# Combining only the two chosen experts of an image, fetched from a table in HBM at addresses computed on the chip

## The chip, the core and the metric

One Trainium2 chip, one of its NeuronCores. The kernel is one launch; its metric is the device time of that launch in microseconds (us). The engines of the core run their own instruction lists and meet only at semaphores: TensorE (PE, with its weight loads shown as PEld), VectorE (DVE), ScalarE (ACT), GpSimd (POOL) and SyncE (SP), whose list holds almost nothing but DMA issues.

## The reference

Input x is 32 images of 32x32 pixels and 64 channels, float32. Two blocks follow one another, each `x = x + block(group_norm(x))`.

```
for t in range(3):                        # block 1: routed convolution, three steps
    attn    = softmax(q . (x Wk)) over pixels, 2 heads
    logits  = pooled(attn, x Wv) @ Wmlp    # 4 experts
    weights = softmax(where(allowed, logits, -1e9) / 1.5)
    top     = the 2 largest of the 4;  wsel = weights of the top 2, normalised, 0 for the others
    x_mod   = x * (1 + mean attention map * 1024 * softplus(alpha))
    x       = sum over e of wsel[e] * (conv3x3(x_mod, We[e]) + be[e])
    allowed = allowed minus the first choice (expert 3 stays allowed)
# block 2: per pixel a 3x3 kernel for each of 16 channel groups from a 64->16 projection, applied to x Wi + bi
```

Since a convolution is linear in its weights, the sum over experts can be formed on the weights first: one combined 3x3x64x64 kernel per image and step, two of whose four terms are zero.

## The kernel before

All 32 images stay in SBUF, two to a tile of 128 partitions (a pair). Four images, that is two pairs, make a quad. A step of the routed block takes 8 quads, cut into two phases of 4 quads, so that there are 6 phases p and 24 quads q = 4p + j. One pass of the main loop does, for quad q: the 3x3 convolution on PE, meanwhile on the other engines the combined weights of quad q+1, its modulated and padded input, and piece by piece the attention and the routing of phase p+1.

Quads 4, 6, 8, 10, 12 and 14 (`SHORT`) use a row transform with 4 forms of the kernel's rows in place of 3 and save a third of the matmuls; their combined weights are 4 blocks of 192 columns (768), those of the others 9 taps of 64 (576). PSUM has two units for the convolution (`conv`, halves h = 0 and 1) and two for everything beside it (`att`).

The combination works as follows. `experts` (128 x 4 x 768) holds the weights of the four experts in both halves of the partitions. `begin_combine(q)` on ACT (L839 to L858) writes expert 0 times its weight into `comb[q % 2]`, once for each pair n; it first waits until the convolution of quad q-2 has read that buffer. `combine(q)` on DVE (L1260 to L1278) adds experts 1, 2 and 3: six `scalar_tensor_tensor`. In a quad with j = 3 behind a short one (`hurried`) DVE also does the first product of pair 0 itself. `comb_added` counts the additions; the convolution waits for them.

The order on each engine is the order of the code. On ACT a pass is: `begin_combine(q+1)`, the exponentials of phase p+1 if j = 0, `copy_middle(q)` if q is short, `round_attention` if j = 2 or 3, then the emptying of the convolution's PSUM. On DVE (L1433 to L1480): `combine(q+1)`, `row_max` and `weigh` if j = 0, `middle_rows(q)` if q is short, `reduce_attention` if j = 3, `modulate(q+1)`, `finish_rows(q, 0)`, and the sums and differences of rows if q+1 is short. The last stage of attention for the next phase (`attention_map` on PE, (3, 1, 2)) waits for `parts_ready`, which ACT raises at the end of `round_attention`.

The routing of phases 0 and 1 is done on DVE (`route`, L1133), that of phases 2 to 5 on POOL (`route_beside`, L1576), one short dependent instruction after the other. SP is idle between the loading of the inputs and the constants of the second block (L388), which it issues when quad 18 has been modulated.

## Time and profile before

| | |
|---|---|
| device time, three runs | 682.75, 683.7, 683.96 us; median 683.7 |
| profiled execution, first to last instruction | 680.8 us |
| granted TensorE clock, mean over the span | 0.985 |
| PE / DVE / ACT / POOL busy | 649.5 / 553.8 / 285.0 / 172.3 us |

The profile gives no separate total of its execution: its span of 680.8 us is 2.9 us below the median of the runs, which is what lies before the first and after the last instruction together with the scatter of single runs. In time the kernel falls in four parts: loading, first norm and routing (0 to about 60 us), quads 0 to 3 (to 130), quads 4 to 23 (to 459), and the second block (to 681). Times of day in the rows are microseconds from the start of the span.

### The profile page before, as it was taken

Reading aid. Unit: us, or ns where it says so; the run is one execution under the profiler, and the core shown is the slowest. Engines: PE = TensorE matmul, PEld = TensorE weight load, DVE = VectorE, ACT = ScalarE, POOL = GpSimd, SP = SyncE. Lnnn points to the kernel's source line nnn. Section 1 sums busy time; section 2 is a strip of 40 time slices with the busy share of each in tenths; the row PEclk is TensorE's granted clock in tenths of the full one; section 3 lists DMA queues with packets and bytes.
Section 4 is the critical chain, followed back from the end, with each engine's and each line's share of the span. In section 5 each row is a group of like instructions: output and inputs, shape, how many; then the busy total and the mean of one; then the engine's idle time right before and its main releaser. Section 6 shows DMA issues by size and latency. Waiting matters only on the chain.

```text
span 680.8 us, 14823 instructions
## 1 busy us (share of the span) xinstructions
PE 649.5 (95%) x6176; PEld 268.1 (39%) x6176; DVE 553.8 (81%) x904; ACT 285.0 (42%) x367; POOL 172.3 (25%) x156
## 2 busy tenths in 40 slices
PE   7878999999999999999999999999999999999995
PEld 7433333333333333333333334433445444444442
DVE  5698866989988988995577787849888888888885
ACT  3753622322331322133002411033676777777661
POOL 2100310009102800550051110411353243244230
PEclk9979999999999999999999999998999999999998
DMA  9920000000000000000000000000111211121122
GB/s 332 213 56 1 2 1 1 1 1 2 2 1 1 2 1 1 2 1 1 1 14 2 1 1 2 1 1 1 32 33 32 58 37 33 45 49 33 32 62 63
DMA packets 54511, 19.67 MB, mean 29 GB/s; under 512 B 51154, under 2 KB 51892, under 8 KB 54452
## 3 DMA queue, kind: packets, MB, share of 16 engines
q1 hardware_dynamic: 54164, 18.57, 11.2%
q8 instruction: 49, 0.80, 0.5%
q10 hardware_dynamic: 288, 0.21, 0.1%
q14 instruction: 10, 0.08, 0.0%
HBM read 10.39 MB, written 8.39 MB: 28 GB/s over the span
## 4 chain that ended last, share of the span: by engine, by line
PE 74%; DVE 15%; issue 1%; ACT 1%; DVEq 0%; ACTq 0%
PE conv L675 35%; PE att L745 11%; PE conv L729 10%; PE att L465 4%; PE conv L641 4%; PE att L544 4%; DVE xpad L1188 3%; DVE comb L1277 2%; PE att L717 2%; DVE stats L1291 2%; PE att L556 2%; DVE x L1497 2%; PE att L523 1%; DVE x L1246 1%; DVE x L1253 1%
## 5 line engine op out<-in xcount | busy, mean ns | idle before, releaser
L675 PE MATMUL conv<-xpad,comb 64*64 64x512 f32 x2592 | 290.3, 595 | 3.1 <-DVE x L1253 2.9
L1497 DVE TENSOR_TENSOR x<-conv,x 128x512 f32<-128x512 f32 x288 | 179.2, 683 | 26.4 <-PE conv L729 25.0
L675 PEld LDWEIGHTS conv<-xpad,comb 64*64 64x64 f32 x2592 | 99.3, 134 | 170.1 <-issue 159.4
L1277 DVE SCALAR_TENSOR_TENSOR comb<-experts,wsel,comb 128x576 f32<-128x576 f32 (+1 forms) x138 | 113.5, 888 | 5.2 <-ACT comb L857 4.8
L729 PE MATMUL conv<-rstack,wse 98*128 98x512 f32 x288 | 96.2, 444 | 1.9 <-DVE xin L1286 0.9
L857 ACT ACTIVATE comb<-experts,wsel 128x576 f32<-128x576 f32 (+2 forms) x49 | 35.2, 768 | 108.5 <-PE conv L675 69.7
L745 PE MATMUL att<-x,cmp 64*32 64x512 f32 x1280 | 79.7, 596 | 0.0
L729 PEld LDWEIGHTS conv<-rstack,wse 98*128 98x128 f32 x288 | 49.5, 189 | 60.7 <-DVE x L1497 46.2
L1188 DVE SCALAR_TENSOR_TENSOR xpad<-att,x 128x1024 f32<-128x1024 f32 x46 | 54.0, 1215 | 20.8 <-PE att L523 20.6
L1634 POOL TENSOR_TENSOR x<-x,xin 128x1024 f32<-128x1024 f32 x15 | 35.9, 2396 | 115.1 <-ACT x L997 115.1
L867 ACT ACTIVATE x<-conv,bias 128x512 f32<-128x512 f32 x40 | 25.2, 680 | 84.0 <-PE conv L675 84.0
L1573 POOL TENSOR_TENSOR rt<-rt 128x16 f32<-128x16 f32 x12 | 6.9, 579 | 199.3 <-ACT rt L837 198.7
L977 ACT ACTIVATE x<-att,small 64x512 f32<-64x512 f32 x64 | 44.0, 687 | 12.6 <-PE att L556 12.0
L1291 DVE BATCH_NORM_STATS2 stats<-xin 128x6 f32<-128x512 f32 x64 | 43.5, 680 | 2.8 <-ACT xin L820 1.4
L1627 POOL TENSOR_TENSOR rstack<-x,rstack 32x1024 fp32r<-32x1024 f32 x16 | 38.1, 2383 | 28.9 <-ACT rstack L989 28.9
L1286 DVE SCALAR_TENSOR_TENSOR xin<-conv,bias,xin 128x512 f32<-128x512 f32 x32 | 22.5, 744 | 26.4 <-PE conv L675 26.1
L997 ACT ACTIVATE x<-att 64x512 f32<-64x512 f32 x60 | 35.5, 592 | 15.8 <-PE att L745 14.7
L641 PE MATMUL conv<-row_sums,comb 64*64 64x512 f32 x288 | 33.3, 591 | 1.3 <-DVE row_sums L1222 1.3
L641 PE MATMUL conv<-xpad,comb 64*64 64x512 f32 x288 | 33.6, 596 | 0.0
L745 PEld LDWEIGHTS att<-x,cmp 64*32 64x32 f32 x1280 | 18.5, 106 | 34.2 <-issue 33.0
L544 PE MATMUL att<-x,wr 128*96 128x512 f32 x64 | 31.5, 615 | 0.0
L1004 ACT ACTIVATE comb<-att 128x1024 f32<-128x1024 f32 x15 | 15.4, 1027 | 31.1 <-PE att L717 31.1
(187 smaller groups left out, 611.4 us busy)
## 6 DMA issues: line engine op xcount, KB each, us to landing
x<-in_x SPq DMA_DIRECT2D x32, 256.0 KB, 5.1
out<-comb SPq DMA_DIRECT2D x30, 256.0 KB, 3.2
experts<-in_We SPq DMA_DIRECT2D x1, 1152.0 KB
out<-comb SPq DMA_DIRECT2D x4, 128.0 KB, 2.2
wide<-in_c_wide SPq DMA_DIRECT2D x1, 192.0 KB, 5.9
x<-in_c_sum SPq DMA_DIRECT2D x1, 160.0 KB
small<-in_c_small ACTq DMA_DIRECT2D x1, 142.5 KB, 3.8
map_sel<-in_c_map SPq DMA_DIRECT2D x1, 128.0 KB
```

The costliest lines, as they stand in the source:

```text
L544: last = nc.tensor.matmul(att[0:rows, 1, cols], weights, xn[s][:, cols], start=True, stop=True)
L641: last = nc.tensor.matmul(conv[own[to], h, HW * rows:HW * rows + HW], comb[own[rows], q % 2, n, form * ROW + kw * C:form * ROW + kw * C + ...
L675: last = nc.tensor.matmul(conv[own[to], h, HW * rows:HW * rows + HW], comb[own[rows], q % 2, n, tap(t)], xpad[own[rows], 2 * (q % 2) + n, ...
L729: nc.tensor.matmul(conv[:, unit, cols], wse[:, ORDER[i], :], rstk[s][0:RR, cols], start=True, stop=True).then_inc(exp_full, 1)
L745: last = nc.tensor.matmul(att[q, 0, bank], sum_sel[own_rows, t + upper, :], prod[i][own_rows, cols], start=(r == 0), stop=(r == len(ROUNDS ...
L977: done = nc.scalar.activation(xip[s][own[n], 1 + 16 * h:17 + 16 * h, 1:W + 1], att[rows, 1, bank].rearrange("p (a b) -> p a b", b=W), ACT. ...
L1188: v.scalar_tensor_tensor(inner(q, n), img(att[:, use.unit, :]), 1.0, img(x[:, slot(q, n), :]), ALU.add, ALU.mult).then_inc(att_free[use.un ...
L1277: v.scalar_tensor_tensor(comb[:, q % 2, n, cols], experts[:, e, cols], wsel[:, p % 2, j + QP * n, e:e + 1], comb[:, q % 2, n, cols], ALU.m ...
L1291: gn.then(v.bn_stats(stats[:, k, n, :], xin[:, k, n * HW:(n + 1) * HW]))
L1497: v.tensor_tensor(img(prod[i])[:, rows, :], img(conv[:, unit, :])[:, rows, :], xip[s][:, kh + 16 * h:kh + 16 * h + 16, kw:kw + W], ALU.mul ...
L1627: v.tensor_tensor(rstk[s][32:64, :], r96[32:64, :], rstk[s][32:64, :].bitcast(F32), ALU.subtract)\
L1634: v.tensor_tensor(fin, fin, xin[:, k, :], ALU.add).then_inc(fin_ready, 1)
```

## The change

From quad 5 on (`GATHER_FROM`) DVE and ACT combine two experts per image and not four.

- POOL computes one more block of rows (`minus_forms`), and SP writes all forms of all four experts into a table `forms` in HBM, 7 blocks of 192 columns for each expert, in three DMAs.
- The routing also gives, for each image, the numbers of its first and second choice (`top_at`, int32) and their weights (`top_weight`): `pick_experts(1)` on DVE for phase 1, new lines in `route_beside` on POOL for phases 2 to 5.
- `gather(q)` on SP: for each of the 4 images of the quad and each of its 2 choices, `value_load` reads the number from SBUF into a register, and a DMA with that address fetches 64 partitions x 576 (or 768) floats into `chosen`, the same memory as `experts`. It overwrites what the quad before used, so it waits for that quad's additions.
- ACT's product waits for the DMAs of its pair and reads the first choice; DVE adds the second: 2 `scalar_tensor_tensor` per quad in place of 6. In short quads the form that DVE used to subtract (`minus_ready`) comes ready from the table.

```
+        top_at = packed(small, 0, 2 * GP * TOP).bitcast(mybir.dt.int32).rearrange("p (a i r) -> p a i r", a=2, r=TOP)
+        chosen = experts[:, :, :].rearrange("p (n r) c -> p n r c", n=2)
+        forms = nc.dram_tensor("forms", (K, C, FORM_BLOCKS * ROW), F32, kind="Internal")
...
+        def added(q):
+            return (K - 1) * (2 + min(q, GATHER_FROM - 1) + 1) + max(0, q - GATHER_FROM + 1)
...
+            def write_forms():
+                eng.wait_ge(forms_ready, 4)
+                table = forms[:, :, :].rearrange("k p c -> p k c")
+                eng.dma_start(table[:, :, 4 * ROW:7 * ROW], experts[0:C, :, 0:3 * ROW]).then_inc(forms_out, 16)
+                eng.dma_start(table[:, :, ROW:4 * ROW], experts[0:C, :, ROW:4 * ROW]).then_inc(forms_out, 16)
+                eng.dma_start(table[:, :, 0:ROW], minus_forms[0:C, :, :]).then_inc(forms_out, 16)
+            def gather(q):
+                p, j = divmod(q, QP)
+                if j == 0 or q == GATHER_FROM:
+                    eng.wait_ge(top_ready, p)
+                first, size = (0, 4 * ROW) if q in SHORT else (4 * ROW, TAPS * C)
+                for n in range(2):
+                    if q == GATHER_FROM:
+                        for m in range(2):
+                            eng.wait_ge(comb_added[m], added(q - 1))
+                    else:
+                        eng.wait_ge(comb_added[n], added(q - 1))
+                    for m in range(2):
+                        for r in range(TOP):
+                            at = eng.value_load(top_at[64 * m:64 * m + 1, p % 2, j + QP * n, r:r + 1], min_val=0, max_val=K - 1)
+                            eng.dma_start(chosen[own[m], n, r, 0:size],
+                                          forms[bass.ds(at, 1), :, first:first + size].rearrange("k p c -> (k p) c")).then_inc(gathered[n], 16)
+            write_forms()
+            eng.wait_ge(forms_out, 16 * FORMS_WRITTEN)
+            for q in range(GATHER_FROM, QP * LAST + 4):
+                gather(q)
             modulated(eng, QP * LAST + 2)
             for dst, src in LATE_CONSTS:
                 eng.dma_start(dst, src).then_inc(late_consts_in, 16)
+            for q in range(QP * LAST + 4, QUADS):
+                gather(q)
...
                 for cols in taps:
                     for n in range(int(hurried(q)), 2):
-                        nc.scalar.activation(comb[:, q % 2, n, cols], experts[:, 0, cols], ACT.Identity,
-                                             scale=wsel[:, p % 2, j + QP * n, 0:1]).then_inc(comb_begun[n], 1)
+                        if q >= GATHER_FROM:
+                            eng.wait_ge(gathered[n], 64 * (q - GATHER_FROM + 1))
+                            first, weight = chosen[:, n, 0, cols], top_weight[:, p % 2, j + QP * n, 0:1]
+                        else:
+                            first, weight = experts[:, 0, cols], wsel[:, p % 2, j + QP * n, 0:1]
+                        nc.scalar.activation(comb[:, q % 2, n, cols], first, ACT.Identity, scale=weight).then_inc(comb_begun[n], 1)
...
+            def combine_two(q):
+                if hurried(q):
+                    eng.wait_ge(conv_full, sections(q - 2, 1))
+                    eng.wait_ge(gathered[0], 64 * (q - GATHER_FROM + 1))
+                    v.tensor_scalar(comb[:, q % 2, 0, cols], chosen[:, 0, 0, cols], weight(0, 0), None, ALU.mult)\
+                        .then_inc(own_begun, 1)
+                for n in range(2):
...
+                    v.scalar_tensor_tensor(comb[:, q % 2, n, cols], chosen[:, n, 1, cols], weight(n, 1),
                                            comb[:, q % 2, n, cols], ALU.mult, ALU.add).then_inc(comb_added[n], 1)
...
             route(1)
+            pick_experts(1)
             next_mask_and_bias(1)
             combine(4)
...
-                        combine(q + 1)
+                        combine_two(q + 1)
```

On SP, behind the input loads, stood the constants of the second block (`in_c_sum` and what follows):

```order
L372 DMA x<-in_x 128x8x64 [waits turn_full]
L372 DMA x<-in_x 128x8x64
L372 DMA x<-in_x 128x8x64 [waits turn_full]
L372 DMA x<-in_x 128x8x64
L390 DMA x<-in_c_sum 128x320 [waits att_free1,att_free0]
L390 DMA x<-in_bs 2x144
L390 DMA x<-in_Ws 16x144 x6
```

Now the table and the gathers stand between them. `TENSOR_LOAD` is the register load of `value_load`, `small` holds `top_at`, and the two kinds of `ISA` are register operations:

```order
L416 DMA forms<-experts 64x4x576 [waits forms_ready]
L417 DMA forms<-experts 64x4x576
L418 DMA forms<-row_sums 64x4x192
L434 TENSOR_LOAD small [waits comb_added_a,comb_added_b,top_ready,forms_out]
L434 ISA x2
L435 ISA
L435 DMA experts<-forms 64x576
L434 TENSOR_LOAD small
L434 ISA x2
L435 ISA
L435 DMA experts<-forms 64x576
```

The four rows from one `TENSOR_LOAD` to the next repeat 152 times, 8 for each of the 19 quads from 5 on; 15 quads stand ahead of `in_c_sum`, 4 behind it.

On DVE, at the routing of phase 1, ahead of the combination of quad 4 (L1277), stood:

```order
L1153 TENSOR_SCALAR rs<-rs 128x8
L1154 RECIPROCAL rs<-rs 128x8
L1155 TENSOR_TENSOR wsel<-rt,rs 128x32
L1160 TENSOR_SCALAR rt<-rt 128x32
L1161 TENSOR_TENSOR rt<-allowed,rt 128x8x3
L1162 TENSOR_SCALAR pack<-rt 128x8x3
L1164 TENSOR_TENSOR rt<-wsel,small 128x32
L1166 TENSOR_REDUCE pack<-rt 128x8
L1277 SCALAR_TENSOR_TENSOR comb<-experts,wsel,comb 128x768 x6
```

Now (L1218 is the old L1155, L1223 the old L1160; the rest follows as before):

```order
L1217 RECIPROCAL rs<-rs 128x8
L1218 TENSOR_TENSOR wsel<-rt,rs 128x32
L1236 TENSOR_SCALAR cmp<-rt 128x8x4
L1237 TENSOR_SCALAR cmp<-rt 128x8x4
L1238 TENSOR_TENSOR cmp<-cmp,small 128x8x8
L1239 TENSOR_TENSOR cmp<-cmp 128x8x2x2
L1240 TENSOR_TENSOR small<-cmp 128x16
L1242 TENSOR_TENSOR cmp<-cmp,wsel 128x8x8
L1243 TENSOR_REDUCE small<-cmp 128x16
L1223 TENSOR_SCALAR rt<-rt 128x32
```

Seven short instructions (L1236 to L1243) have moved in between; the combination of quad 4 still has six additions.

## Rows read from the trace of the kernel before

**Rows 1.** The page: busy time, 40 slices of the span

```profile
PE 649.5 (95%) x6176; PEld 268.1 (39%) x6176; DVE 553.8 (81%) x904; ACT 285.0 (42%) x367; POOL 172.3 (25%) x156
...
PE   7878999999999999999999999999999999999995
```

**Rows 2.** Windows: stretch, length, busy us (instructions) of PE, PEld, DVE, ACT, POOL, clock, DMA

```profile
252.00:315.40 63.40, 61.92 (x593) 21.86 (x586) 55.88 (x72) 18.54 (x27) 18.16 (x24) 1.00 0.00 1
315.40:380.00 64.60, 64.60 (x614) 22.33 (x610) 40.42 (x61) 11.51 (x16) 11.43 (x24) 1.00 0.02 5
```

**Rows 3.** Timeline of weight loads, 150 to 215: start, length, idle before and releaser

```profile
174.11 0.24 PEld L641 LDWEIGHTS conv<-xpad,comb 64*64 64x64 f32 x8 [0.82 <-issue]
...
177.57 0.21 PEld L675 LDWEIGHTS conv<-xpad,comb 64*64 64x64 f32 x8 [1.46 <-DVE x L1253]
...
187.82 0.35 PEld L523 LDWEIGHTS att<-parts,map_sel 64*64 64x64 bf16 x8 [0.48 <-issue]
...
212.75 0.21 PEld L675 LDWEIGHTS conv<-xpad,comb 64*64 64x64 f32 x8 [1.21 <-DVE x L1253]
```

**Rows 4.** Timeline of DVE, 116 to 150, quads 3 and 4

```profile
119.38 0.19 DVE L1155 TENSOR_TENSOR wsel<-rt,rs 128x32 f32<-128x32 f32 x1
...
120.62 5.66 DVE L1277 SCALAR_TENSOR_TENSOR comb<-experts,wsel,comb 128x768 f32<-128x768 f32 x6
...
138.93 1.21 DVE L1070 TENSOR_REDUCE soft<-att 128x1 f32<-128x1024 f32 x1
...
141.60 1.23 DVE L1079 SCALAR_TENSOR_TENSOR att<-attn,att 128x1024 f32<-128x1024 f32 x1 [1.27 <-ACT attn L832]
...
143.46 1.22 DVE L1245 TENSOR_TENSOR x<-x,conv 128x1024 f32<-128x1024 f32 x1
```

**Rows 5.** Timeline of PE, 130 to 192, quads 4 to 7

```profile
138.63 4.52 PE L641 MATMUL conv<-row_sums,comb 64*64 64x512 f32 x40
...
149.38 1.95 PE L675 MATMUL conv<-xpad,comb 64*64 64x512 f32 x16 [0.56 <-DVE x L1253]
...
182.77 0.25 PE L534 MATMUL att<-pack,ident 64*64 64x16 f32 x8
```

**Rows 6.** Timeline of DVE, 150 to 180, quads 5 and 6

```profile
152.70 5.66 DVE L1277 SCALAR_TENSOR_TENSOR comb<-experts,wsel,comb 128x768 f32<-128x768 f32 x6
...
166.40 0.51 DVE L1265 TENSOR_SCALAR comb<-experts,wsel 128x576 f32<-128x576 f32 x1
166.94 4.75 DVE L1277 SCALAR_TENSOR_TENSOR comb<-experts,wsel,comb 128x576 f32<-128x576 f32 x6
171.64 1.22 DVE L1245 TENSOR_TENSOR x<-x,conv 128x1024 f32<-128x1024 f32 x1
```

**Rows 7.** Timeline of ACT, 150 to 193

```profile
168.64 1.26 ACT L877 ACTIVATE x<-conv,bias 128x512 f32<-128x512 f32 x2 [0.65 <-PE conv L641]
...
186.65 1.06 ACT L892 ACTIVATE parts<-attn 128x1024 bf16<-128x1024 f32 x1 [5.71 <-DVE attn L1258]
```

**Rows 8.** Source line L395 on SP: ns min/median/max of the store loop's instructions

```profile
L395 SPq DMA_DIRECT2D out<-comb x30: 541/542/674, 489.3 to 671.1; - x30
L395 SPq FUSED_REGOPS  x28: 52/55/67, 489.1 to 659.0; - x28
L395 SPq MOVE out<-comb x28: 29/29/29, 489.2 to 659.1; - x28
```

**Rows 9.** DMA issues: KB each, median us from issue to landing

```profile
out<-comb SPq DMA_DIRECT2D x30, 256.0 KB, 3.2
...
out<-comb SPq DMA_DIRECT2D x4, 128.0 KB, 2.2
```

**Rows 10.** Timeline of POOL, 150 to 192, routing of phase 2

```profile
162.33 1.17 POOL L1593 TENSOR_TENSOR rt<-cmp 128x32 f32<-128x32 f32 x1
...
172.86 0.21 POOL L1605 TENSOR_TENSOR pack<-rt 128x8 f32<-128x8 f32 x1
```

**Rows 11.** Lines: the products of ACT

```profile
L857 ACT ACTIVATE comb<-experts,wsel 128x576 f32<-128x576 f32 (+2 forms) x49 | 35.2, 768 | 108.5 <-PE conv L675 69.7 <-PE conv L641 35.0 <-DVE wsel L1155 3.7
```

More of the change, by code:

```diff
@@ L111 @@
 CUT = H // 2 + 1
-SMALL = (4 + K) * D + 29
+SMALL = (4 + K) * D + 29 + K
+TOP = 2
+GATHER_FROM = QP + 1
+FORM_BLOCKS = 7
+FORMS_WRITTEN = 3
 EARLY = GP + 5
@@ L344, in hurried, with hurried_upto @@
             return q - 1 in SHORT and q % QP == QP - 1
+        def hurried_upto(q):
+            return sum(hurried(k) for k in range(q + 1))
+        def added(q):
+            return (K - 1) * (2 + min(q, GATHER_FROM - 1) + 1) + max(0, q - GATHER_FROM + 1)
         def modulated(eng, q):
@@ L1166, in next_mask_and_bias, with pick_experts @@
                 v.tensor_reduce(pack[:, p % 2, :, 0], rt[:, 2, :, :], AX.X, ALU.add).then_inc(pack_ready, 1)
+            def pick_experts(p):
+                ranked = [128, GP, TOP, K]
+                own_rank, taken, half = cmp[:, 0, :, 0:TOP, :], cmp[:, 1, :, 0:TOP, :], cmp[:, 2, :, 0:TOP, 0:2]
+                pk = Steps(eng, pick_step)
+                v.tensor_scalar(own_rank[:, :, 0, :], rt[:, 5, :, :], 0.5, None, ALU.is_lt)
+                pk.then(v.tensor_scalar(own_rank[:, :, 1, :], rt[:, 5, :, :], 1.0, None, ALU.is_equal))
+                pk.then(v.tensor_tensor(taken, own_rank, ramp.unsqueeze(1).unsqueeze(1).to_broadcast(ranked), ALU.mult))
+                pk.then(v.tensor_tensor(half, taken[:, :, :, 0:2], taken[:, :, :, 2:4], ALU.add))
+                v.tensor_tensor(top_at[:, p % 2, :, :], half[:, :, :, 0], half[:, :, :, 1], ALU.add).then_inc(top_ready, 1)
+                eng.wait_ge(top_ready, p)
+                pk.then(v.tensor_tensor(taken, own_rank, bc(wsel[:, p % 2, :, :], 2, ranked), ALU.mult))
+                v.tensor_reduce(top_weight[:, p % 2, :, :], taken, AX.X, ALU.add).then_inc(top_weighed, 1)
             def permuted(p):
@@ L1229, in subtract_rows @@
                 pads = xpad[:, 2 * (q % 2):2 * (q % 2) + 2, :, :]
-                for n in range(2):
-                    eng.wait_ge(comb_added[n], (K - 1) * (2 + q + 1))
-                    v.tensor_tensor(comb[:, q % 2, n, 0:ROW], comb[:, q % 2, n, 3 * ROW:4 * ROW], comb[:, q % 2, n, 0:ROW],
-                                    ALU.subtract).then_inc(minus_ready, 1)
+                if q < GATHER_FROM:
+                    for n in range(2):
+                        eng.wait_ge(comb_added[n], added(q))
+                        v.tensor_tensor(comb[:, q % 2, n, 0:ROW], comb[:, q % 2, n, 3 * ROW:4 * ROW], comb[:, q % 2, n, 0:ROW],
+                                        ALU.subtract).then_inc(minus_ready, 1)
                 eng.wait_ge(sums_ready, 2 * SHORT.index(q) + 2)
@@ L1262, in combine @@
                 cols = slice(0, 4 * ROW if q in SHORT else TAPS * C)
+                for e in range(1, K):
+                    for n in range(2):
+                        if e > 1:
+                            eng.wait_ge(comb_added[n], (K - 1) * (2 + q) + e - 1)
+                        else:
+                            eng.wait_ge(comb_begun[n], 2 + q + 1)
+                        v.scalar_tensor_tensor(comb[:, q % 2, n, cols], experts[:, e, cols], wsel[:, p % 2, j + QP * n, e:e + 1],
+                                               comb[:, q % 2, n, cols], ALU.mult, ALU.add).then_inc(comb_added[n], 1)
@@ L1263, in combine, with weight @@
+            def combine_two(q):
+                p, j = divmod(q, QP)
+                cols = slice(0, 4 * ROW if q in SHORT else TAPS * C)
+                def weight(n, r):
+                    return top_weight[:, p % 2, j + QP * n, r:r + 1]
                 if hurried(q):
                     eng.wait_ge(conv_full, sections(q - 2, 1))
-                    v.tensor_scalar(comb[:, q % 2, 0, cols], experts[:, 0, cols], wsel[:, p % 2, j, 0:1], None, ALU.mult)\
+                    eng.wait_ge(gathered[0], 64 * (q - GATHER_FROM + 1))
+                    v.tensor_scalar(comb[:, q % 2, 0, cols], chosen[:, 0, 0, cols], weight(0, 0), None, ALU.mult)\
@@ L1266, in combine @@
                         .then_inc(own_begun, 1)
-                steps = [(e, n) for e in range(1, K) for n in range(2)]
-                if hurried(q):
-                    steps = [(1, 0), (2, 0), (1, 1), (3, 0), (2, 1), (3, 1)]
-                for e, n in steps:
-                    if e > 1:
-                        eng.wait_ge(comb_added[n], (K - 1) * (2 + q) + e - 1)
-                    elif hurried(q) and n == 0:
-                        eng.wait_ge(own_begun, p)
-                    else:
-                        eng.wait_ge(comb_begun[n], 2 + q + 1 - (0 if n else sum(hurried(k) for k in range(q))))
-                    v.scalar_tensor_tensor(comb[:, q % 2, n, cols], experts[:, e, cols], wsel[:, p % 2, j + QP * n, e:e + 1],
+                for n in range(2):
+                    if hurried(q) and n == 0:
+                        eng.wait_ge(own_begun, hurried_upto(q))
+                    else:
+                        eng.wait_ge(comb_begun[n], 2 + q + 1 - (0 if n else hurried_upto(q - 1)))
+                    v.scalar_tensor_tensor(comb[:, q % 2, n, cols], chosen[:, n, 1, cols], weight(n, 1),
```

41 lines of the change are left out of this document (35 added, 6 removed).

## The prediction

> **What bounds the kernel now.** I read the page's busy shares first, then the windows by stage, then the idle time of the weight loads, and last the timeline of DVE, ACT and POOL around each place where PE waits. PE is busy 95% of the span and DVE 81%, and from quad 4 on PE stands at nine tenths or more in nearly every slice [rows 1]. The windows say it more sharply: in a phase with short quads PE works 61.9 of 63.4 us and DVE 55.9; in phase 4 PE works 64.6 of 64.6 and DVE only 40.4 [rows 2]. So DVE, from which the change takes work, is not what the routed block lasts as long as. What is left to win are PE's true stalls, best seen where the idle time of a weight load exceeds the 0.28 to 0.30 us that lie between all of them: in a phase 0.5 us in the middle of a quad with j = 2 (0.82), 1.2 us behind it (1.46), 0.9 us behind the one with j = 0 (1.21), and 0.2 us at the attention map (0.48) [rows 3]. The longest are released by DVE's L1253, but the chain in front of it is L1245, L1246, two L1188 and L1253, which starts when PE has finished the middle rows, and the change touches none of these. Only two stalls depend on the combination at all: at j = 2 it ends at 166.94 + 4.75 = 171.69 and L1245 starts at 171.64, just as the middle rows are ready [rows 6], and the map waits for ACT's last rounding, which ends at 186.65 + 1.06 = 187.71 [rows 7].
>
> **What it removes.** 19 quads lose four additions each, about 60 us of DVE, and short ones two subtractions. Cover: PE's own work. What it can return is 0.2 us at the map in two phases and at most 0.06 at each of three quads with j = 2: -0.5 us. Behind a short quad L1245 is late next, by PE itself.
>
> **pick_experts(1).** Seven DVE instructions of 8 to 64 elements. From L1155 to L1277 six of their like start every (120.62 - 119.38)/6 = 0.21 us [rows 4]; I take 0.22, since more of these wait for the one before: 1.54 us. They stand on the path: DVE comes to the additions of quad 4 at 120.62, their last ends at 126.28 [rows 4], then come modulation and row sums, on which PE waits to begin quad 4. PE is never ahead again, so all of 1.54 us counts at that place.
>
> **The first gather.** It can start when quad 4's last addition has freed the buffer: 126.28 + 1.54 = 127.8. SP then does eight times: register load, two register operations, address, DMA issue. The store loop shows the issue with a register address: 0.54 us, 0.055 for the FUSED_REGOPS and 0.03 for the MOVE [rows 8]; with 0.055 each for the two operations behind the load a step is s = T + 0.74, where T is the load. No row shows T. From below it is a register operation without memory, 0.03 us; from above a whole DMA to its landing, 2.2 us [rows 8, 9]. It has to reach SBUF and come back, so it should exceed the 0.54 us of an issue by the same sequencer, the nearest row; I take 0.8, half as much again, and s = 1.54, 8s = 12.3. A DMA of 144 KB lands between the 2.2 us of 128 KB and the 3.2 of 256 KB [rows 9]; I take 2.4 after the start of its issue. The last block of pair 1 is then there at 127.8 + 12.3 - 0.54 + 2.4 = 142.0.
>
> Behind it hangs a chain: ACT's product 0.77 [rows 11], one addition 0.8, then in DVE's order row_max (from its start to weigh's 141.60 - 138.93 = 2.67, with ACT's exponentials between), 1.86 to L1245 at 143.46, and 5.92 from there to PE's start of quad 5 at 149.38 [rows 4, 5]. Sum 12.05 with a semaphore's 0.03: quad 5 starts at 154.1 and not at 149.38. In general it is 8s - 7.6 later; the 1.54 us above is in it. It has a floor: L1245 can't start before the middle rows, 138.63 + 4.52 + 1.54 = 144.7 [rows 5], which is 1.2 late. With s = 1.54: +4.7 us. PE has nothing else to do there, since stage 3 of quad 4 waits for the same L1246.
>
> *The Trainium skill on this.* "DMA: Bandwidth & Descriptors", section "Latency and other measured facts", gives a register load ("tensor_load") a floor of about 600 ns. By that s would be 1.34, the first gather +3.1 and the total 686.3 us; no run here shows it yet. Nothing above rests on it.
>
> **The later gathers.** A phase lasts 212.75 - 149.38 = 63.4 us [rows 3, 5], 15.8 per quad. SP needs 8s = 12.3 of them. What counts is whether a gather, which can start only behind the additions of the quad before, lands before ACT or DVE, in their order, owe PE something else:
> - j = 3 (quads 7, 11, 15), shown at quad 7 in times of the old trace: pair 0 of quad 6 is added at 152.70 + 0.94 [rows 6]; landing 153.64 + 8s + 1.86. ACT then has its product and copy_middle, 0.77 + 1.26 [rows 7, 11], ahead of L1245 at 171.64. It holds up to 8s = 14.1, s = 1.76. Here: 167.8, early by 1.8.
> - j = 0 (8, 12, 16), shown at quad 8: start 166.40 + 0.51 + 0.8 = 167.7, when quad 7's pair 0 is added [rows 6]; landing 169.6 + 8s; then product 0.88, rounding 1.06, DVE's L1258 1.28, rounding 1.06, for the map that PE takes at 187.8 [rows 3, 7]. It holds up to s = 1.72. Here: 186.2.
> - all others have more room, and in phases 4 and 5 a gather may be later than PE's start of the quad before by most of 16 us. The eight constants' DMAs among them are 0.54 each at most, 4.3 us of SP once, with room too.
>
> **The routing on POOL** grows by nine instructions. Six precede the numbers: at 1.17 us at the most (L1593) and 0.21 at the least (L1605) [rows 10], I take 0.5 and 3 us: numbers at 163.5 + 3 = 166.5, before 167.7. The next mask, ready at 173.1, moves to 177.6, at worst 183.6, and PE wants it at 182.77 [rows 5, 10]. Nothing. Traffic: 8 x 144 KB per quad, 1.2 MB in 15.8 us, on DMA engines with a share of 0.00 to 0.02 [rows 2]. Nothing. The extra block of row forms and the table are written long before DVE's first row sum at some 130 us. Nothing.
>
> **The sum.** +4.7 - 0.5 = +4.2 us. The profiled execution's span of 680.8 becomes 685.0; the median of the runs lies 2.9 above the span, so 683.7 becomes 687.9 us.
>
> **Rivals.**
> - *The load is a long round trip.* T = 1.37, midway between issue and landing: s = 2.11. First gather +9.3. Quads with j = 3: 8 x (2.11 - 1.76) = 2.8 late, three times, 8.4. Quads with j = 0: SP is free only at 170.5, numbers land at 189.2, rounding ends at 193.5 against 187.8 + 2.8: 2.9, three times, 8.7. Together +26, 710 us. For it: nothing in the trace shows a load to be as cheap as an issue. Against: it carries 4 bytes and no completion. The Trainium skill ("Runtime: NRT & Kernel Launch", "The ~15µs preamble/postamble breakdown") has about 1.3 us for register loads at launch, from HBM; by that T the same sum gives some 707 us.
> - *SP becomes the engine that all wait for.* With T at its upper bound s is 2.94 and a quad costs SP 23.5 us. The 19th gather ends at 127.8 + 19 x 23.5 = 574 where PE began quad 23 at 440: about 820 us. It decides from 8s = 16, s = 2.0, gradually. Against it: the same as above, more strongly.
> - *Not slower.* With T up to 0.45, s below 1.2, the first gather hides up to the floor, +1.2 - 0.5: 684.4 us. If besides the middle rows are really ready earlier than the modelled ends of matmuls let one see, the six additions of old held the quads with j = 2 back, and each gives up to the difference between its stalls (0.5 + 1.2) and those of j = 0 (0.1 + 0.9), 0.7: -2.1 us, 682.3. For it: combination and L1245 touch without a gap [rows 6]. Against: so do PE and L1245 at j = 0, where the combination is long over.
>
> That the fetch doesn't take place is no rival: the order shows 152 of them.
>
> **How the numbers follow.** Forecast (s from 1.2 to 1.75, +1.4 to +6.5, its own range 685 to 690): 54%. Long load (up to 712 and a little over): 20%. SP-bound: 9%. Not slower: 17%, of it 12 within 0.2% and 5 faster. 0.2%, 1.4 us, is about what measurements of this kernel can tell from none; the three runs differ by 1.2 us. The range of 8 in 10 reaches from the lower case to the long load: 683 to 712. Faster 0.05, same 0.13 (a sliver of the forecast's lower end is in it), slower 0.82.
>
> **What would show it.** DVE busy falls by some 55 to 60 us and PE's stays near 649 while the span grows. SP's line of the register load gives T: 0.8. Quad 5 starts 4 to 5 us later than 149.4, with ACT's L857 (its successor) released by a DMA, and the phases behind it are 63.2 to 63.4 us long as before. Wrong: phases longer than 64 us (then a j = 3 or j = 0 gather is late, or SP-bound if every quad is stretched), quad 5 on time, or a phase shorter than 62.5 us, which would mean that DVE did hold PE.

## The result, and the profile after

| | kernel before | changed kernel |
|---|---|---|
| median of the runs, us | 683.23 (682.68 to 683.96, 4 runs) | 686.62 (686.3 to 686.84, 4 runs) |
| span of the profiled execution, us | 680.8 | 684.9 |

The ratio is 1.0054, 95% interval 1.004 to 1.0068: slower by 3.4 us. The forecast was 687.9 us in a range of 683 to 712, with a chance of 0.82 for slower. Two executions that took far longer at a low granted clock, one of the kernel before (1118.34 us, clock 0.557, beside e1, e2, e4 and c1) and one of c4 (844.89 us, clock 0.748), are left out of all comparisons.

The page of the changed kernel, its busy times, answers to [rows 1]:

```profile
PE 650.6 (95%) x6176; PEld 267.8 (39%) x6176; DVE 496.1 (72%) x825; ACT 286.1 (42%) x367; POOL 174.3 (25%) x193
```

DVE works 57.7 us less than in [rows 1], PE about as much (650.6 against 649.5), and the span is 4.1 us longer: DVE's time was not what the kernel lasts as long as.

SP's two lines of the gather, ns min/median/max, and below them the time from issue to landing:

```profile
L434 SPq TENSOR_LOAD <-small x152: 267/354/716, 128.0 to 425.2; - x152
L434 SPq FUSED_REGOPS  x152: 152/152/185, 128.5 to 425.5; - x152
L434 SPq SEQ_ASSERT  x152: 18/18/33, 128.7 to 425.7; - x152
...
L435 SPq FUSED_REGOPS  x152: 37/46/51, 128.8 to 425.8; - x152
L435 SPq MOVE experts<-forms x152: 29/29/38, 128.9 to 425.9; - x152
L435 SPq DMA_DIRECT2D experts<-forms x152: 468/469/851, 129.0 to 425.9; - x152
...
DMA to landing us min/median/max: 2.4/2.7/3.8
```

The medians add up to 1.07 us. The step is longer: the eight issues of the first gather start from 128.97 to 139.41, that is 1.49 us each; the rest lies in the longer ones of the loads (in these eight steps they are short and long by turns) and in the gaps between the instructions.

Timeline of DVE, with pick_experts(1) (L1236 to L1243) and the combination of quad 5 (L1370). It answers to [rows 4]:

```profile
119.74 0.19 DVE L1218 TENSOR_TENSOR wsel<-rt,rs 128x32 f32<-128x32 f32 x1
119.97 0.18 DVE L1236 TENSOR_SCALAR cmp<-rt 128x32 f32<-128x32 f32 x1
...
121.24 0.22 DVE L1243 TENSOR_REDUCE small<-cmp 128x16 f32<-128x64 f32 x1
...
122.21 5.66 DVE L1349 SCALAR_TENSOR_TENSOR comb<-experts,wsel,comb 128x768 f32<-128x768 f32 x6
...
142.89 0.82 DVE L1370 SCALAR_TENSOR_TENSOR comb<-experts,small,comb 128x576 f32<-128x576 f32 x1 [5.28 <-ACT comb L921]
143.62 1.22 DVE L1133 TENSOR_REDUCE soft<-att 128x1 f32<-128x1024 f32 x1
...
146.30 1.23 DVE L1142 SCALAR_TENSOR_TENSOR att<-attn,att 128x1024 f32<-128x1024 f32 x1 [1.27 <-ACT attn L888]
...
148.16 1.21 DVE L1325 TENSOR_TENSOR x<-x,conv 128x1024 f32<-128x1024 f32 x1
```

The chain of the prediction stands there link by link. ACT's product, the old L857 of [rows 11], waits for the last block:

```profile
142.08 0.78 ACT L921 ACTIVATE comb<-experts,small 128x576 f32<-128x576 f32 x1 [5.32 <-DMA experts<-forms]
```

then come one addition, row_max, weigh and L1325 (L1245 of before). PE in the same stretch, against [rows 5]:

```profile
133.19 5.34 PE L521 MATMUL att<-x,sw 128*32 128x512 f32 x32 [0.37 <-DVE allowed L1251]
138.35 3.62 PE L521 MATMUL att<-x,uw 128*32 128x512 f32 x32
141.89 4.52 PE L697 MATMUL conv<-row_sums,comb 64*64 64x512 f32 x40
...
154.08 1.95 PE L731 MATMUL conv<-xpad,comb 64*64 64x512 f32 x16 [0.58 <-DVE x L1333]
```

Quad 5 starts at 154.08, where [rows 5] have 149.38: 4.70 us later. From there to the second block nothing is lost and nothing won: PE's first weight load of that block that waits for its input stands at 464.95, before at 460.25, which is 310.87 us behind quad 5's start in both. Windows from one start of a j = 1 quad to the next, after; the columns are those of [rows 2]:

```profile
154.08:217.44 63.36, 61.88 (x586) 21.77 (x586) 43.53 (x53) 18.49 (x27) 17.44 (x33) 1.00 0.32 89
```

The same phase had 63.37 us before ([rows 5] to the last row of [rows 3]), and DVE works 43.53 of them where it did 57.08. At the very end the weight load of PE's last transposes (679.05, before 674.35) still stands 4.70 us behind the old one. Of the 4.70, 0.36 came from ahead of the change: L1218, L1155 of before, starts at 119.74 and in [rows 4] at 119.38, a scatter of single executions: in eleven of the twelve traces below the same instruction starts between 119.19 and 119.75, in e4 at 121.39. And 0.6 us are given back behind the start of these last weight loads, where only transposes, ACT, DVE and stores are left: to the end of the span there are 5.85 us, before 6.45. Most of this is scatter too (6.03 and 6.04 in e3 and e7, which fetch nothing; 5.63 to 5.69 in nine of the ten that fetch, 6.02 in c1); what makes the remaining 0.3 to 0.4 us is not shown.

One thing the prediction has nowhere: L521's first 32 matmuls take 5.34 us and the next 32, of the same shape, 3.62. The windows show what differs (first row: the kernel before; second: the changed kernel):

```profile
134.00:136.00 2.00, 2.00 (x24) 0.57 (x20) 2.00 (x3) 0.00 (x0) 0.00 (x0) 1.00 0.00 0
```

```profile
134.00:136.00 2.00, 2.00 (x16) 0.65 (x12) 2.00 (x2) 0.01 (x1) 0.00 (x0) 0.50 0.27 78
```

The granted clock is 0.50, the lower level of 1.2 GHz. What went ahead of it: PE waits for quad 4's row sums, which the pick makes later. The weight load's idle time there, before and after:

```profile
130.07 0.24 PEld L641 LDWEIGHTS conv<-row_sums,comb 64*64 64x64 f32 x8 [2.18 <-issue]
```

```profile
131.63 0.24 PEld L697 LDWEIGHTS conv<-row_sums,comb 64*64 64x64 f32 x8 [3.38 <-issue]
```

So quad 4's middle rows, 1.56 us late by then, are 3.26 late at L697 (141.89 against 138.63). They are ready at 141.89 + 4.52 = 146.41, L1325 starts only at 148.16. So here it costs nothing, since the gather's chain comes later still. The experiments separate the two.

### The profile page after: what moved, and what is told of

Same layout as the page of the kernel before. It is cut to its first block, busy times and chain, and to the rows that moved or that the text cites. A ratio compares the mean times of both kernels' runs of the same rounds, so it can differ in the third digit from the quotient of the medians.

```text
span 684.9 us, 15720 instructions
## 1 busy us (share of the span) xinstructions
PE 650.6 (95%) x6176; PEld 267.8 (39%) x6176; DVE 496.1 (72%) x825; ACT 286.1 (42%) x367; POOL 174.3 (25%) x193
## 4 chain that ended last, share of the span: by engine, by line
PE 69%; DVE 8%; issue 2%; SPq 1%; DMA 0%; ACT 0%; DVEq 0%
PE conv L731 32%; PE att L801 11%; PE conv L785 10%; PE conv L697 4%; PE att L600 4%; PE att L521 3%; DVE xpad L1265 2%; PE att L773 2%; PE att L612 2%; DVE x L1591 2%; DVE x L1326 1%; PE att L579 1%; DVE x L1333 1%; SPq L434 1%; SPq L435 1%
## 5 line engine op out<-in xcount | busy, mean ns | idle before, releaser
L1591 DVE TENSOR_TENSOR x<-conv,x 128x512 f32<-128x512 f32 x288 | 179.2, 683 | 26.5 <-PE conv L785 25.2
L921 ACT ACTIVATE comb<-experts,small 128x576 f32<-128x576 f32 (+1 forms) x35 | 27.8, 818 | 130.2 <-PE conv L731 71.7
L1670 POOL TENSOR_TENSOR rt<-rt 128x16 f32<-128x16 f32 x12 | 4.9, 407 | 202.3 <-ACT rt L893 201.6
L1370 DVE SCALAR_TENSOR_TENSOR comb<-experts,small,comb 128x576 f32<-128x576 f32 (+1 forms) x38 | 32.0, 867 | 18.4 <-ACT comb L921 18.3
L697 PE MATMUL conv<-row_sums,comb 64*64 64x512 f32 x288 | 33.2, 591 | 2.5 <-DVE row_sums L1301 2.5
L697 PE MATMUL conv<-xpad,comb 64*64 64x512 f32 x288 | 33.7, 597 | 1.2 <-ACT x L940 1.2
L1632 POOL TENSOR_TENSOR rstd<-variance,mhalf 128x4 f32<-128x4 f32 (+1 forms) x6 | 8.9, 1488 | 77.6 <-DVE variance L1124 77.6
```

The source lines that it names most:

```text
L697: last = nc.tensor.matmul(conv[own[to], h, HW * rows:HW * rows + HW], comb[own[rows], q % 2, n, form * ROW + kw * C:form * ROW + kw * C + ...
L1591: v.tensor_tensor(img(prod[i])[:, rows, :], img(conv[:, unit, :])[:, rows, :], xip[s][:, kh + 16 * h:kh + 16 * h + 16, kw:kw + W], ALU.mul ...
```

## The experiments

All times are medians; a ratio is to the kernel before in runs on the same chip. Where a trace of a single execution is read, differences within it are sharper than those of the medians; a table at the end of this section has one such difference for every run.

**Is DVE's relief worth anything?** e3 takes work from DVE without fetching:

```
- steps = [(e, n) for e in range(1, K) for n in range(2)]
+ steps = [(e, n) for e in range(1, K if q <= QP else 2) for n in range(2)]
```

> The kernel before, which from quad 5 on leaves out the additions of experts 2 and 3 (their part of the sum is missing): DVE is relieved of four additions in each of 19 quads, as by the change, with no gather, table or added routing. Theory A (PE bounds, DVE's relief returns nothing): 683.2 us within 0.6. Rival (DVE holds PE back somewhere, and the change gave that back against a larger cost of its own): 682 us or less.

Measured: 682.52 us (681.89 to 683.89, 11 runs), ratio 1.0002 [0.9993, 1.0011]. Experts 2 and 3 are left out of the sums from quad 5 on, and the kernel takes the same time. PE's stall behind the middle rows of quad 6 is as long as in [rows 3], so it doesn't come from the additions:

```profile
177.45 0.21 PEld L679 LDWEIGHTS conv<-xpad,comb 64*64 64x64 f32 x8 [1.46 <-DVE x L1257]
```

The one place where the relief shows is the start of quad 5, where the weight load stands idle for 1.21 us and not 1.44.

e7 instead puts the next quad's map and modulation ahead of the middle rows, in the kernel before:

```
- elif at == ((2, 0) if j == 0 else (1, 1)):     (PE: where the map stands)
+ elif at == ((2, 0) if j == 0 else (0, 1) if q >= 0 else (1, 1)):
...
+ if q in SHORT and j == 2: modulate(q + 1)
  if q in SHORT: middle_rows(q)
...
- modulate(q + 1)
+ if not (q in SHORT and j == 2): modulate(q + 1)
```

> The kernel before with the map and the modulation of the next quad ahead of the middle rows in quads 6, 10 and 14. DVE has no room for it there: its combination ends at 171.7, when the middle rows are ready. Theory A: L1245 is 2.4 us later and PE's next quad 1.5 us later, three times: +4.6, 687.8 us. If it were faster than before, the early modulation would need no relief of DVE, and a gain of the kernel that has both would not be the change's.

Measured: 687.70 us (686.87 to 688.77, 4 runs), ratio 1.008 [1.0064, 1.0095], as expected. The additions now end where the modulation has to be over; PE then waits 3.04 us at each of the three places:

```profile
167.03 4.75 DVE L1277 SCALAR_TENSOR_TENSOR comb<-experts,wsel,comb 128x576 f32<-128x576 f32 x6
171.70 2.34 DVE L1188 SCALAR_TENSOR_TENSOR xpad<-att,x 128x1024 f32<-128x1024 f32 x2
```

```profile
176.42 0.24 PEld L641 LDWEIGHTS conv<-xpad,comb 64*64 64x64 f32 x8 [3.04 <-issue]
```

So the relief is worth nothing in the order of before, but it opens an order that was closed.

**Which part of the first gather costs?** e1 starts the fetching one quad later (`GATHER_FROM = QP + 2`); quad 5 gets its six additions back. So it keeps the pick, but not the first gather's chain at quad 5.

> Only GATHER_FROM moves, from quad 5 to quad 6: 18 gathers remain of 19. Theory A (the loss is one chain at quad 5, whose gather lands late and holds row_max, exponentials, weigh and L1245, +3.1 us, and pick_experts on DVE's path, +1.2 us; all else is hidden): the 3.1 us go, quad 5 starts at about 151 us and the time is before +1.2 to +1.5, some 684.6 us. Theory B (each gather, its traffic and the longer routing cost a little everywhere): one nineteenth of the loss goes, 686.4 us.

Measured: 684.28 us (682.85 to 685.44, 8 runs), ratio 1.0021 [1.0011, 1.0032]: A. Quad 5 starts at 151.82. The idle time is again 3.38 us and the clock falls again:

```profile
132.00:134.00 2.00, 1.63 (x20) 0.58 (x16) 1.80 (x6) 0.00 (x0) 0.00 (x0) 0.61 0.00 0
134.00:136.00 2.00, 2.00 (x12) 0.39 (x8) 2.00 (x3) 0.00 (x0) 0.00 (x0) 0.54 0.00 0
```

With nothing of the gather in its way, this is what the pick costs: quad 5 is 2.44 us late, by 1.2 us of DVE and some 1.5 us of half clock (from L521's start at 132.85 to L697 at 141.31 are 8.46 us, before from 131.63 to 138.63 only 7.00), less the 0.2 us that e3 showed at this start.

e2 keeps the gather at quad 5 and moves row_max(2), weigh(2) and the exponentials ahead of quad 5's combination, so that only one product and one addition hang behind the last block:

```
+ if q == QP: exponentials(p + 1)          (ACT, ahead of begin_combine(q + 1))
...
+ if q == QP: row_max(p + 1); weigh(p + 1)    (DVE)
  combine_two(q + 1)
- if j == 0 and attended: ...
+ if j == 0 and q > QP and attended: ...
```

> All 19 gathers stay; in quad 4 alone row_max and weigh of phase 2 stand ahead of quad 5's combination on DVE, and the exponentials ahead of its product on ACT. Theory A: the gather's landing at 142 us then holds back only the product and one addition, which end at 143.7, ahead of L1245's floor of 144.7 to 145; the time is before +1.3 to +1.6, some 684.7 us. Theory B: 686.6 us as the changed kernel.

Measured: 686.89 us (685.35 to 688.26, 6 runs), ratio 1.0056 [1.0042, 1.007]. A failed in its number, not in its chain. The chain is gone: L1327 (L1325 of the changed kernel) now waits for PE, not for a block. But quad 5 starts at 153.32, 0.76 us sooner and no more (0.24 of it are scatter from ahead of the change: L1220, the old L1155, starts at 119.50), because the half clock lasts longer in this run (0.74 in 130 to 132, then 0.50, 0.50, 0.55) and L697 starts at 142.81:

```profile
147.40 1.22 DVE L1327 TENSOR_TENSOR x<-x,conv 128x1024 f32<-128x1024 f32 x1 [0.97 <-PE conv L697]
```

And all of it is lost again at quad 8's attention map:

```profile
193.18 0.17 PEld L579 LDWEIGHTS att<-parts,map_sel 64*64 64x64 bf16 x8 [1.90 <-issue]
```

The edit itself has a part in this. In the changed kernel pair 0 of quad 5 is added at 136.79; in e2 both pairs wait behind weigh and are added at 144.89, and only then may quad 6's gather overwrite their blocks. ACT's second product for quad 6 waits for it, and the exponential of phase 2's routing (L893) stands behind that product, at 161.33 where the changed kernel has it at 157.52:

```profile
160.49 0.94 ACT L921 ACTIVATE comb<-experts,small 128x768 f32<-128x768 f32 x1 [5.73 <-DMA experts<-forms]
161.33 0.21 ACT L893 ACTIVATE rt<-rt 128x32 f32<-128x32 f32 x1
```

e8 has the same wait at the map, and e9 tests this cause of it.

**Can the pick be had for nothing?** e8 is e1 with pick_experts(1) between row_max(2) and weigh(2), where DVE waited 1.27 us for ACT [rows 4]:

```
- pick_experts(1)                     (ahead of next_mask_and_bias(1))
  row_max(p + 1)
+ if p == 1: pick_experts(1)
  weigh(p + 1)
```

> As in e1 the two chosen experts alone are combined from quad 6 on, but VectorE does pick_experts(1) only in quad 4's step, between row_max(2) and weigh(2), where it stood idle for 1.27 us waiting for ScalarE. In e1 the seven instructions stood ahead of quad 4's additions, the row sums were 1.2 us later, the weight load then stood idle for 3.4 us, and the granted clock was at 0.5 to 0.6 for over 3 us behind that. A (the pick and the clock are all that e1 pays): the idle time of the weight load ahead of quad 4 is back at 2.2 us, the clock stays at 1.00 from 128 to 140 us, quad 5 starts at 149.4 to 149.9 instead of 151.8, and the whole is within 0.5 us of the kernel before: ratio 1.0 to 1.001. B (the first gather, or fetching as such, has a price too): quad 5 may be on time, but later quads shift and the whole stays over 1 us above the kernel before, ratio 1.0015 or more, as e1.

Measured: 684.13 us (682.66 to 685.12, 11 runs), ratio 1.0022 [1.0013, 1.0031]. A is right on everything up to quad 7 and wrong on the whole. The idle time of the weight load is 2.17 us, the clock 1.00, and quad 5 starts on time:

```profile
149.30 0.21 PEld L731 LDWEIGHTS conv<-xpad,comb 64*64 64x64 f32 x8 [1.46 <-DVE x L1333]
...
189.05 0.17 PEld L579 LDWEIGHTS att<-parts,map_sel 64*64 64x64 bf16 x8 [1.80 <-issue]
```

But the map has the wait of e2. ACT's timeline shows its origin:

```profile
156.11 0.94 ACT L921 ACTIVATE comb<-experts,small 128x768 f32<-128x768 f32 x1 [5.59 <-DMA experts<-forms]
156.95 0.21 ACT L893 ACTIVATE rt<-rt 128x32 f32<-128x32 f32 x1
...
184.64 0.94 ACT L921 ACTIVATE comb<-experts,small 128x768 f32<-128x768 f32 x1 [5.05 <-DMA experts<-forms]
```

L893 is the exponential of phase 2's routing. It stands behind quad 6's products in ACT's list, and these wait for the first gather. In the kernel before it started at 152.8. The gather is late in part by the pick's new place: its first issue, at 142.18, has to wait for the numbers, which DVE has at 141.10, where quad 5's additions end at 138.89. POOL's routing starts 4 us late with it, the numbers are there at 170.47 (L1699 at 170.27 + 0.20), and quad 8's gather, its product at 184.64 and the rounding behind it are late for the map. In the changed kernel L893 isn't held up (157.52, right behind its input), and the numbers of 170.44 serve a PE that is 4.7 us late itself: the last rounding ends at 190.80, the map comes at 192.30.

**e9** is e8 with that one instruction ahead of the products:

```
+ if q + 1 == GATHER_FROM: route_exp(p + 1)
  begin_combine(q + 1)
```

> As e8, but in quad 5's step ScalarE does the exponential of phase 2's routing (L893) ahead of quad 6's two products, which in e8 waited for the first gather's blocks: L893 started at 156.95 us where it had its input at 152.7. A (the wait at the map in e8 comes from there: exponential late, GpSimd's routing late, numbers at 170.5, quad 8's gather late): L893 at 152.9, numbers at about 166.4, quad 8's gather starts at about 167.5 instead of 170.5 and is complete at about 181.6, the weight load at the attention map stands idle for 0.3 to 0.5 us instead of 1.80, and the whole falls by 1.2 us: 682.9 us, ratio 1.0007. B (quad 8's gather is late because SP itself or quad 7's additions are late): L893 is early, the map still waits 1.5 us or more, ratio 1.002 as in e8.

Measured: 682.17 us (681.78 to 683.18, 11 runs), ratio 0.9989 [0.998, 0.9998]: A. ACT, POOL and the weight load at the map:

```profile
153.22 0.23 ACT L893 ACTIVATE rt<-rt 128x32 f32<-128x32 f32 x1 [10.12 <-DVE rt L1195]
...
181.78 0.94 ACT L921 ACTIVATE comb<-experts,small 128x768 f32<-128x768 f32 x1 [3.40 <-DMA experts<-forms]
```

```profile
163.84 1.24 POOL L1701 CAST small<-cmp 128x16 int32<-128x16 f32 x1
```

```profile
188.02 0.13 PEld L579 LDWEIGHTS att<-parts,map_sel 64*64 64x64 bf16 x4 [0.28 <-issue]
```

The map waits no longer. Quads 5 to 8 take 63.38 us (149.78 to 213.16) against 64.51 in e8 (149.30 to 213.81): 1.13 us, what A had. That the medians differ by 2 us is not all its doing: in e8's trace the second block, which the edit doesn't touch, takes 221.09 us at a granted clock of 0.83 from 660 to 670, in e9's 219.75 at 1.00. So 18 quads are fetched at no cost, pick included; the changed kernel's loss is in how its first gather and its pick are placed.

**Later starts.** e5 fetches from quad 8 (`GATHER_FROM = 2 * QP`), e4 from quad 10 (`2 * QP + 2`), both without pick_experts(1), the numbers coming from POOL alone; `combine`, which now has quad 7 to do with four experts again, is the one of the kernel before.

> Gathers from quad 8 on, no pick_experts. Gather 8 can start only when both pairs of quad 7's full combination are added, at 171.7 us of the old trace, and lands some 13.5 us later at 185.3; product, two roundings and DVE's step between them take 4.3: 189.6 against PE's attention map at 187.8. Theory A with its deadline at quads with j = 0: +1.8 us, 685.0 us, with the weight load of that map idle for about 2 us more. Rival (the deadline is not where I put it): 683.2 us, as with gathers from quad 10 on.

Measured: 686.55 us (684.38 to 686.72, 5 runs), ratio 1.0054 [1.004, 1.0068]. The mechanism is A's, its size is larger. The map waits 3.41 us:

```profile
190.57 0.17 PEld L579 LDWEIGHTS att<-parts,map_sel 64*64 64x64 bf16 x8 [3.41 <-issue]
```

A first gather waits for the additions of both image pairs of the quad before (171.7), a later one only for those of its own pair; its eighth issue starts at 183.08 and its block is there only at 186.1, 0.8 us behind the 185.3 expected. In this trace quads 5 to 8 take 66.14 us, 2.77 more than before where A had 1.8. The profiled execution took 684.38, the least of the five; why the others (685.0 to 686.72) took longer no trace shows.

> Gathers from quad 10 on (14 of them), no pick_experts on DVE, the table and the longer routing on POOL stay. Theory A: nothing of the two terms is left and the 14 gathers are hidden: the time of the kernel before, 683.2 us, within 0.4. Theory B: 14 of 19 parts of the 3.4 us stay, 685.7 us. If the relief of DVE were worth something by itself it would show here as a time below 682.5.

Measured: 682.14 us (681.59 to 683.78, 11 runs), ratio 0.999 [0.9982, 0.9999]: A. That quad 10 is a j = 2 quad doesn't decide it, since e8's quad 6 is one too. Here the numbers are long there, the first issue is at 204.06 and the last product at 217.42, so that L893 behind it comes at 218.26: no later than in the kernel before (216.18) in an execution that is 2.0 us late already ahead of the routing of phase 1.

**Does the step decide?** e6 doubles each register load, so that the step s grows and nothing else.

> The changed kernel with each register load done twice: a gather step of 1.43 us becomes some 1.98. Theory A with all its deadlines: first gather +4.4 more, quads 7, 11, 15 late by 8 x (1.98 - 1.76) = 1.8 each, quads 8, 12, 16 by some 2 each, together some 15 us more than the changed kernel, 700 us. Rival (only the first gather is near a deadline): 691 us. Rival B (a cost for each of 152 loads on the path): 152 x 0.55 = 84 us, 770 us.

Measured: 712.82 us (712.26 to 713.27, 4 runs), ratio 1.0442 [1.0426, 1.0458]; eight issues from 129.05 to 143.44, s = 2.06. No expectation fits, A by 13 us. The first places are A's, the middle of quad 4, quad 7's gather and the map of quad 8:

```profile
151.54 0.34 PEld L698 LDWEIGHTS conv<-xpad,comb 64*64 64x64 f32 x8 [8.20 <-issue]
...
184.76 0.33 PEld L698 LDWEIGHTS conv<-xpad,comb 64*64 64x64 f32 x8 [3.34 <-issue]
...
203.85 0.17 PEld L580 LDWEIGHTS att<-parts,map_sel 64*64 64x64 bf16 x8 [2.41 <-issue]
```

One thing that A left out stands behind the first two: the clock at its lower level again.

```profile
150.00:154.00 4.00, 2.43 (x16) 1.06 (x20) 3.57 (x8) 1.43 (x4) 0.00 (x0) 0.50 0.34 98
154.00:158.00 4.00, 4.00 (x27) 1.31 (x24) 3.08 (x4) 0.00 (x0) 0.00 (x0) 0.56 0.34 98
184.00:188.00 4.00, 3.21 (x16) 1.17 (x20) 3.56 (x4) 2.74 (x4) 0.00 (x0) 0.60 0.34 93
```

The other is a place: the map of quad 20, in the phases without short quads, waits 4.04 us (at 414.38), with the clock at 0.50 from 414 to 420. By the starts of quads 5, 9, 13, 17 and of the second block the 26.5 us over the changed kernel are 6.0 at quad 5 (A: 4.4), 14.2 in the three phases behind it (A: 11.4) and 6.2 at quad 20 (A: nothing). The rival of the prediction with s = 2.11 had 710 us, and its nearness to 712.8 is luck in part: it had 9.3, 17.1 and nothing over the kernel before, the trace 10.7, 14.2 and 6.2. The run shows how little room there was: 0.57 us more per step cost 26 us.

**What the relief can buy.** c1 is e4 with e7's early modulation in quads 10 and 14, where DVE now has the time:

> As the kernel that gathers from quad 10 on, and in quads 10 and 14 the attention map and the modulation of the next quad stand ahead of the middle rows (map behind the second tap of stage 0). Theory A: DVE is free there for some 2.6 us since it adds two experts and not four; the modulation leaves the chain behind the short quad, PE is held only by the middle rows, and each of the two quads wins 0.9 us: 681.4 us. Rival: the gather's second pair lands too late, the modulation pushes L1245 back by a microsecond or more, and it is no faster than 683.2 us.

Measured: 680.65 us (680.1 to 682.19, 6 runs), ratio 0.997 [0.9957, 0.9982]. The modulation fits in ahead, and L1325 waits for PE:

```profile
232.49 2.35 DVE L1265 SCALAR_TENSOR_TENSOR xpad<-att,x 128x1024 f32<-128x1024 f32 x2
235.27 1.22 DVE L1325 TENSOR_TENSOR x<-x,conv 128x1024 f32<-128x1024 f32 x1 [0.44 <-PE conv L697]
```

Against e4 that is 1.5 us for two quads, where the same edit cost 5.2 us for three in e7. c3 is e8 and c4 is e9 with it in quads 6, 10 and 14.

> As e8 (chosen experts alone from quad 6, pick_experts(1) in VectorE's idle time), and in quads 6, 10 and 14 the next quad's map and modulation go ahead of the middle rows on ScalarE and VectorE. The room for that is what the change gave VectorE; in quads 10 and 14 it gave 1.5 us against the version without (c1 against e4). A: quad 6 gives 0.7 more, so that the whole is 680.0 us where the kernel before has 682.6, ratio 0.9965. B (in quad 6 the gather for quad 7 lands too late for an early modulation): quad 6 gives nothing or takes 0.5, ratio 0.9975 or more, no better than c1.

Measured: 681.29 us (680.76 to 685.06, 12 runs), ratio 0.9988 [0.9977, 0.9999]: B on the whole. In its trace quads 5 to 8 take 63.97 us, 0.54 less than in e8 and 0.60 more than before: the map of quad 8 still waits, 2.06 us.

> As e9, and in quads 6, 10 and 14 the next quad's map and modulation ahead of the middle rows. A: the map of quad 8 no longer waits (2.06 us of idle weight load in c3), which is worth 1.4 to 1.7 us: 679.6 us, ratio 0.9962, the fastest so far by a microsecond. B: ratio 0.998 or more, as c3.

Measured: 680.62 us (679.98 to 683.29, 11 runs), ratio 0.9971 [0.9961, 0.998]. A is half right. The map doesn't wait; but quad 6 gives nothing, since the block for quad 7 comes 1.34 us after ACT is free for its product:

```profile
168.54 0.78 ACT L921 ACTIVATE comb<-experts,small 128x576 f32<-128x576 f32 x1 [1.34 <-DMA experts<-forms]
```

```profile
174.81 0.24 PEld L697 LDWEIGHTS conv<-xpad,comb 64*64 64x64 f32 x8 [1.64 <-issue]
```

From quad 5's start to the attention scores in quad 8 (L521) are 45.83 us in c4 (149.26 to 195.09) and 45.83 in e9 (149.78 to 195.61). c4 and c1 are the fastest and equal; c1 has the less delicate placement.

**All runs over the same stretch.** The time from L1155 (`wsel`, 119.38 in the kernel before) to PE's first weight load of the second block that waits for its input (460.25) leaves out what scatters ahead of the change and behind it. It is 340.87 us in the kernel before; in the others, one execution each, it is longer or shorter by:

| changed | e1 | e2 | e3 | e4 | e5 | e6 | e7 | e8 | e9 | c1 | c3 | c4 |
|---|---|---|---|---|---|---|---|---|---|---|---|---|
| +4.34 | +2.45 | +5.04 | -0.24 | -0.03 | +2.76 | +31.33 | +4.73 | +1.17 | +0.03 | -1.61 | -1.01 | -1.59 |

e4 and e9 have the length of before to 0.03 us: what makes their medians 0.5 us shorter than those of before lies outside this stretch. In the traces it is the second block, from that weight load to the end of the span, with 219.77 and 219.75 us against 220.55; that the change is the cause is not shown.

## Why the prediction was right, and where it was not

- *DVE does not bound.* Right: 57.7 us less work, the same phases, and e3 the same time (0.24 us less in the stretch of the table).
- *The term of -0.5 us.* Wrong. The weight load's idle time at the map did go (0.48 in [rows 3], 0.28 now), but the phase stayed at 63.36 us, and at 63.37 in e3. The reading was wrong, not only the size: a weight load that comes late is no stall of PE as long as matmuls are still running. By the profile's ends of matmuls those of L675 that start at 182.86 last until 188.22, and the map's matmuls follow without a gap:

```profile
188.04 0.61 PE L523 MATMUL att<-parts,map_sel 64*64 64x512 bf16 x8
```

In the changed kernel they start at 192.73, 4.69 us later like everything else.
- *pick_experts(1), 1.54 us.* Mis-sized: 1.23 (L1218 to L1349 are 2.47 us, 1.24 in [rows 4]). What the step left out is what hangs on it: PE idle longer, then at half clock, +1.5 to 1.7 us of PE more. In the changed kernel it lies in the gather's shadow; in e1 it is on the path. The prediction's floor of +1.2 was really +2.4 (quad 5 in e1).
- *The first gather, s = T + 0.74 with T = 0.8.* The step s was right, 1.49 against 1.54, its parts not, and that is luck: the load's median is 0.35, less than half of T, and the register operation behind it costs 0.152, not 0.055. With T = 0.35 the formula gives 1.09, the case of the rival "Not slower"; what makes 1.49 of it are the longer loads and the gaps between instructions, for which the sum had no term. The Trainium skill ("DMA: Bandwidth & Descriptors", "Latency and other measured facts") gives a register load a floor of some 600 ns; the trace has 152 of them with a median of 354 and a least of 267, and the measurement decides. That the 686.3 us by that figure lie nearer to 686.62 than mine is luck of the same kind as my own.
- *The chain behind the last block.* Right link by link, with some luck in its start: last block predicted for 142.0 and there by 142.08, 12.00 us from ACT's product to quad 5 against 12.05, quad 5 at 154.08 against 154.1. Four sizes cancel in it: the pick 0.3 less, seven steps 0.3 less, the landing 2.65 from the last issue and not 2.4, and 0.36 of scatter from ahead of the change. Without the latter the shift is 4.3.
- *The later gathers are hidden.* Right here: the last rounding for quad 8's map ends 1.5 us ahead of it (1.6 predicted). But that deadline was drawn with the routing's numbers on time, and with 2.4 us for landings that take 3.0 in short quads (192 KB; 2.6 for 144 KB, medians). What was missing is the instruction queued behind a waiting one on ACT, L893: where quad 6's gather is late, it delays quad 8's by way of POOL (e2, e8). And "all others have more room" fails for quad 20 when s grows to 2.06 (e6).
- *POOL's routing.* Right. The six instructions ahead of the numbers take 1.9 us (L1693 at 168.59 to 170.44), not 3.
- *Traffic and constants at nothing.* Right: the queue moves 26 MB more, a DMA share of 0.32 in a phase instead of 0.01, with PE's phase unchanged.
- *The sum.* Forecast was +4.2. The shift at quad 5 is 4.70 and stays, since the -0.5 is missing; less 0.6 at the end it is the span's +4.1. The step from span to median was mis-sized: wherever both are known, the time is 1.7 to 2.0 us above the span, so of the 2.9 us about 1.0 was scatter of the execution that was profiled. By the same offset that execution took some 682.7 us, 0.5 below the median of 683.23, while the changed kernel's took 686.71, close to its median of 686.62; so the spans differ by 4.1 and the medians by 3.4. The median of the kernel before, taken again beside the changed one, is 683.23 and not 683.7, and from there the same sum gives 687.4.

The rivals: the long load and the SP-bound kernel fall with T. e6 shows what the first would have been, 10.7 us at quad 5 and more behind it, though not in all its places; the second no run tests. "Not slower" had its condition on the load met (0.35, below 0.45) but not that on s (1.49, not below 1.2). It falls for this placement and holds for another: e9 and e4 are within 0.2% of before, on the faster side.

## What to carry to other kernels

When work moves from an engine that is not the bound to a fetch with computed addresses, price the first fetch apart from all others: those behind it run a quad ahead, the first has a path from its numbers through eight serial steps to the consumer. Start it where nothing is due for one step of the loop, make its numbers in a gap of the engine that makes them, and go through what is queued behind each waiting instruction on every engine. The time that the bypassed engine won was worth nothing by itself here; look for an order of its work that it had no room for.

## What the runs showed of the hardware

- A register load from SBUF took SyncE 267 ns at least, 354 in the median and 716 at most (152 loads of the changed kernel), and the whole step with its DMA 1.49 us (2.06 with two loads). The starts of the first gather's issues, 128.97, 130.31, 132.03, 133.27, 135.19, 136.47, 138.17, 139.41, are by turns some 1.3 and 1.7 us apart (once 1.9).
- The granted clock fell to 1.2 GHz for 3 to 7 us after a wait of 3.38 us at quad 4's row sums, in the changed kernel, e1 and e2. It stayed at 1.00 after 2.17 or 2.18 us in before, e4, e8 and e9. The length of the idle time alone doesn't decide it: e6 has the 3.38 us too, and no fall there, but falls with waits of 8.20, 3.34 and 2.98 us (the last at 252.89, clock 0.50 from 254 to 256); the 3.41 us of e5 at the map and the 3.04 us of e7 leave it at 1.00. What does is open.
- Stretches at the lower clock are seen in the weight loads without looking at the clock: idle times of 0.54 to 0.66 us between groups of four instead of 0.28 to 0.30.
